# Cross attention with the sum and reciprocal of the exponentials taken two steps behind the score, and the first stage's output turned back in the banks of the query projection

## The reference, cut to what matters

```python
def _L0_xattn_ref(hidden_states_query, hidden_states_key, attention_mask, Wq, bq, Wk, bk, Wv, bv):
    q = _split_heads(hidden_states_query @ Wq.T + bq)
    k = _split_heads(hidden_states_key @ Wk.T + bk)
    v = _split_heads(hidden_states_key @ Wv.T + bv)
    scores = jnp.einsum('bhqd,bhkd->bhqk', q * scale, k)
    scores = scores + ((1.0 - attention_mask) * -10000.0)[:, None, :, :]
    probs = jax.nn.softmax(scores, axis=-1)
    ctx = jnp.einsum('bhqk,bhkd->bhqd', probs, v)
    return ctx.transpose(0, 2, 1, 3).reshape(b, lq, h * d)

def _L1_xattn_ref(query, key, value, Wq, Wk, Wv, Wo):
    # the same without biases, a causal mask over the 77 keys, and at the end
    return out @ Wo.T

x = x + _L0_xattn_ref(_layernorm(x, axis=-1), ctx_1024, mask, ...)
...
x = x + _L1_xattn_ref(_layernorm(x, axis=-1), ctx_1024, ctx_1024, ...)
```

## Time and profile before

| | |
|---|---|
| median of 3 runs | 5784.02 us (5778.58 to 5785.17) |
| the profiled execution, its own time | 5785.95 us |
| its span, first to last instruction | 5783.8 us |
| PE busy | 5318.4 us, 92% |
| DVE, ACT, POOL busy | 2616.3, 1700.1, 1270.2 us |
| `xa`, first score to last rows written | 808.6 to 1170.1 us of the span |
| `xb`, the same | 3207.1 to 3616.9 us |

### The profile page before, as it was taken

How to read it: one execution, slowest core, us unless ns; L and a number is a source line. 1 busy time by engine, 2 the same in 40 slices (tenths; PEclk the granted TensorE clock), 3 DMA queues, 4 the chain that set the end, 5 groups by cost and what they waited for, 6 DMA issues and landing times. The chain is left out here.

```text
span 5783.8 us, 76040 instructions
## 1 busy us (share of the span) xinstructions
PE 5318.4 (92%) x25936; PEld 2647.4 (46%) x25936; DVE 2616.3 (45%) x4211; ACT 1700.1 (29%) x2290; POOL 1270.2 (22%) x918
## 2 busy tenths in 40 slices
PE   8999978879999899799978899559999999999999
PEld 4444445534445444344444555424444444444444
DVE  3252336544343232254542554655555455455554
ACT  1011024412212100234321333124444444444443
POOL 1010024411112100000002121333333333333333
PEclk9999989979999899899989999579999999999999
DMA  1010021131011222598976010469598745845546
GB/s 54 8 51 0 15 73 48 40 93 43 17 29 59 93 94 87 156 210 200 218 181 220 24 45 23 151 222 341 183 327 284 243 150 157 295 152 198 180 130 236
DMA packets 437257, 770.97 MB, mean 133 GB/s; under 512 B 64386, under 2 KB 207238, under 8 KB 436564
## 3 DMA queue, kind: packets, MB, share of 16 engines
q1 hardware_dynamic: 375892, 724.24, 38.1%
q0 software_dynamic: 34304, 44.13, 3.9%
q10 hardware_dynamic: 26880, 0.19, 0.3%
HBM read 576.17 MB, written 116.79 MB: 120 GB/s over the span
## 5 line engine op out<-in xcount | busy, mean ns | idle before, releaser
L2639 PE MATMUL ex_ps<-ex_w,ex_xT 128*64 128x512 f32 x5376 | 1228.8, 599 | 18.2 <-DVE ex_w L2523 18.2
L2523 DVE COPY ex_w<-ex_shelf 128x4096 f32 x336 | 770.5, 2293 | 522.3 <-PE ex_ps L2639 370.4
L2574 ACT ACTIVATE ex_w<-ex_shelf 128x4096 f32 x168 | 607.8, 3618 | 1044.9 <-PE ex_ps L2655 1011.0
L2639 PEld LDWEIGHTS ex_ps<-ex_w,ex_xT 128*64 128x64 f32 x5376 | 373.6, 138 | 655.9 <-issue 611.6
L2655 PE MATMUL ex_ps<-ex_w,ex_hT 128*64 128x256 f32 x5376 | 610.6, 380 | 5.5 <-ACT ex_hT L2590 3.8
L2493 POOL DMA_INDIRECT out<-ex_y,ex_ix_out x168 | 287.8, 1713 | 1179.0 <-DVE ex_ix L2511 823.6
L2655 PEld LDWEIGHTS ex_ps<-ex_w,ex_hT 128*64 128x64 f32 x5376 | 389.4, 137 | 270.5 <-issue 100.2
L2476 POOL DMA_INDIRECT ex_x<-moe_xn,ex_ix x168 | 410.1, 2441 | 96.5 <-issue 51.4
L1400 PE MATMUL ff_ps<-ff_w,ff_hT 128*128 128x512 f32 x768 | 348.8, 597 | 0.8 <-DVE ff_w L1282 0.8
L1557 PE MATMUL pr_ps<-pr_w,pr_xT 128*128 128x512 f32 x768 | 337.5, 597 | 4.8 <-DMA pr_bias<-L_attn_bq 4.8
L1355 ACT ACTIVATE ff_gT<-ff_ps,ff_bet,ff_gam 128x128 f32<-128x128 f32 x384 | 144.3, 460 | 455.6 <-PE ff_ps L1408 455.6
(11 more groups left out here) (272 smaller groups left out, 7030.3 us busy)
## 6 DMA issues: line engine op xcount, KB each, us to landing
ex_shelf<-L_ffn_w SPq DMA_DIRECT2D x128, 2048.0 KB
ex_shelf<-L_ffn_wo SPq DMA_DIRECT2D x64, 2048.0 KB, 11.5
cv_gt<-cv_g SPq DMA_DIRECT2D x320, 128.0 KB, 3.3
cv_vt<-cv_v SPq DMA_DIRECT2D x256, 128.0 KB, 3.9
ff_x<-x SPq DMA_DIRECT2D x16, 1024.0 KB, 7.9
at_low<-x SPq DMA_DIRECT2D x8, 1024.0 KB, 5.7
x<-at_acc SPq DMA_DIRECT2D x8, 1024.0 KB, 4.2
xa_x<-x SPq DMA_DIRECT2D x8, 1024.0 KB, 7.7
```

Source lines behind the costliest of these rows:

```text
L2523: dve.tensor_copy(w_s[n][:, :], pick(shelf[n], buf)).then_inc(w_set[n].sem, 1)
L2574: act.activation(w_s[2][:, :], pick(shelf[2], buf), ACT.Copy).then_inc(w_set[2].sem, 1)
L2639: mm = pe.matmul(ps[q * G:(q + 1) * G, which, 0:FQ], xT[:, p % 2, k, :], wu[which][:, k, q * FQ:(q + 1) * FQ], start=k == 0, stop=k == KD - 1)
```

## The change

In both stages VectorE takes `total` of step g-2 instead of g-1 ahead of `score(g)`, and GpSimd multiplies by the reciprocal of g-2; both loops run one step longer. In `xa` alone the transposes of `put` write banks 6 and 7, in turn with `project_q`, instead of bank 5, and `add_rows` reads them there. The numbers of buffers, the instructions and their sizes are the same.

```diff
-    LT, LV, LO = 3, 4, 8
+    LS, LT, LV, LO = 2, 3, 4, 8
...
             if g >= LO and (g - LO) % 2 == 0 and (g - LO) // 2 < NT:
-                (wide if gated else side).append(("out", (g - LO) // 2))
+                wide.append(("out", (g - LO) // 2))
...
-            for g in range(G + 1):
-                if g:
-                    s3 = s_sb[:, (g - 1) % SR]
-                    pool.wait_ge(rec_done, g)
-                    pool.tensor_tensor(s3, s3, rec[:, (g - 1) % 2].unsqueeze(2).to_broadcast([P, HB, SK]), ALU.mult).then_inc(mul_done, 1)
+            for g in range(G + LS):
+                v = g - LS
+                if v >= 0:
+                    s3 = s_sb[:, v % SR]
+                    pool.wait_ge(rec_done, v + 1)
+                    pool.tensor_tensor(s3, s3, rec[:, v % 2].unsqueeze(2).to_broadcast([P, HB, SK]), ALU.mult).then_inc(mul_done, 1)
...
-                bank = 6 + wide_at["out", T] % 2 if gated else 5
+                bank = 6 + wide_at["out", T] % 2
...
-                if 1 <= g <= G:
-                    total(g - 1)
+                if LS <= g < G + LS:
+                    total(g - LS)
...
             def put(T):
                 pe.wait_ge(o_done, 2 * T + 2)
-                if gated:
-                    n = wide_at["out", T]
-                    if n >= 2:
-                        pe.wait_ge(*freed(wide, n - 2))
-                    for k in range(KD):
+                n = wide_at["out", T]
+                if n >= 2:
+                    pe.wait_ge(*freed(wide, n - 2))
+                for k in range(KD):
+                    if gated:
                         i = pe.matmul(ps[:, 6 + n % 2, :], oT[:, T % 2, k, :], wo_s[:, k, :], start=k == 0, stop=k == KD - 1)
-                else:
-                    n = side_at["out", T]
-                    pe.wait_ge(*freed(side, n - 1))
-                    for k in range(KD):
-                        i = pe.transpose(ps[:, 5, k * P:(k + 1) * P], oT[:, T % 2, k, :], ident[:, :])
+                    else:
+                        i = pe.transpose(ps[:, 6 + n % 2, k * P:(k + 1) * P], oT[:, T % 2, k, :], ident[:, :])
```

## The result

Four runs of the changed kernel gave 5697.25 to 5703.74 us, median 5702.35, against 5784.6 for the kernel before; the ratio is 0.9856, 95% interval 0.9839 to 0.9873. The profiled execution took 5697.25 us, its span is 5695.3 us.

A forecast was written before the change was run, and what follows sets the result against it. VectorE's ring was taken to bind short steps of `xa`, PE the long ones. Savings of 42.3 + 8.0 + 9.5 + 3.9 in `xa` and 6.7 in `xb`, 70.4 us, took 5784.0 to 5713.6, say 5714; range 5702 to 5742.

The forecast's parts named there:

- The ring: Short steps of `xa`: VectorE's loop through GpSimd's subtraction and the exponential makes a step 4.87 us; PE has 2.8 to 3.4.
- Put's wait: In `xa`, PE waits 11 times, 15.6 us, for the turned tile's copy ahead of put; counted inside the 46 us, not added.
- the excess: Middle chunks of `xa`: 44.55 us against the 36.9 PE needs at full clock, 7.65 us a chunk, 46 over six.
- Rival 5: A projection in `xa` would wait for rows in its bank, PE waiting at L990; given nothing of its own, no chance stated.
- The stall of 0.64 in u3: Fourth step of a middle `xa` chunk: PE stalls 0.64 us for the mask, so a chunk lasts 37.5 us.
- The deductions for a low clock: In `xa`, PE at a lowered clock takes 1.5 us off the first chunk's saving and adds 2.5 to the tail.
- The walk: The new schedule of `xa` followed step by step from PE's first score of a chunk, allowing 0.1 us for each hand-over.
- The unfavourable end: All unfavourable bounds of the stretches of `xa` and `xb` together: a gain of 33 us, time 5751.
- stalls shrink but stay: PE's 12 waits in the middle of `xb`, 14.0 us, each lose only 0.39, 4.7 in all; waits fall from 1.1 to 0.7.
- the tail loses 1.06 us: End of `xb`: rows come before the last sum, so the last step's turn_p starts later, 1.0 us lost.
- Cover of 0.24 us ahead of turn_p: Short steps of `xa`: GpSimd's product ends 0.24 us before PE reaches turn_p; cost put at nothing, bound 7 us.
- rival 4: turn_p waits for its product at L1015 in every short step of both stages: 64 us slower, 5848; chance 2%.

## Why the prediction was right and its size was not

- The ring (mask, maximum, subtraction, exponential, sum) bound the short steps of `xa`, and PE the long ones: right. With the ring open the chunk is 37.01 us, PE's own 36.9; with the sum ahead of the rows, where PE waits nowhere in these chunks, it is 36.85.
- Put's wait: right that it lies inside the excess, shown by the interaction of 18.5 us between the parts (341.4 against 413.7 - 47.2 - 6.6 = 359.9). Rival 5 (the bank move does harm) is out: once the ring is open the move brings 25 us.
- The stall of 0.64 in u3: mis-sized. It was 0.16, since I had added up VectorE's steps from durations: normalise costs 0.45 us from start to start and not 0.62, the rows 0.60 and not 0.69. A chunk became 37.01 instead of 37.5 us; 6 x 0.49 = 2.9 us, the whole miss of the middle chunks.
- The deductions for a low clock, 1.5 us in the first chunk and 2.5 in the tail: this step failed, and it is the largest of the misses. The first was carried over from the first chunk of `xb`, the second from the clock of 0.71 that the tail itself had before. Long pauses stood ahead of the slow instructions in both, in that tail one of 2.41 us and in the first chunk of `xb` these:

```profile
3210.55 0.80 PE L1006 MATMUL xb_ps<-xb_kblk,xb_qT 64*128 64x154 f32 x8 [2.66 <-DVE xb_s L856]
...
3214.69 1.40 PE L1006 MATMUL xb_ps<-xb_kblk,xb_qT 64*128 64x154 f32 x8 [2.76 <-DVE xb_s L856]
```

  In the changed kernel the pauses of the first chunk of `xa` are at most 1.0 us and those of its tail 0.6 to 0.8, and the clock is 1.00 in both stretches:

```profile
807.31 0.80 PE L1007 MATMUL xa_ps<-xa_kblk,xa_qT 64*128 64x154 f32 x8 [0.99 <-DVE xa_s L846]
...
1087.44 1.07 PE L1016 MATMUL xa_ps<-xa_ident,xa_s 128*77 128x128 f32 x8 [0.84 <-ACT xa_pT L952]
```

  The walk without the deductions (34.4 and 14.3) meets the measured 33.95 and 14.06. These 4 us and the 2.9 are 6.9 of the 8.9 by which the terms fell short; the rest is the last chunk (0.7), the walk of the first (0.4) and of the tail (0.2) and `xb` (0.7).
- Not all of the distance is the forecast's. With the 8.9 us put right it would say 5704.7, inside the range; the measured 5700.7 is 4 us lower still, and nothing in the traces ties these 4 us to the change. The interval of the ratio is 10 us to either side.
- The range was built on bounds of both signs, but its lower end allowed only 12 us, and the errors did not cancel: each of the five stretches gained more than was forecast. The unfavourable end was also added up wrongly. The bounds given are 35.3, 4, 6 and 0 in `xa` and -1.0 in `xb`, which make a gain of 44 us (5740), not 33 (5751).
- `xb`: stalls shrink but stay (7.8 us, 12 times), the tail loses 1.06 us against 1.0: right. The sum of 7.4 against 6.7 hides two misses: the middle gained 6.2 instead of 4.7, the first chunk 0.85 instead of 1.8, at a clock that is 0.83 there, lower than before (0.87).
- Cover of 0.24 us ahead of turn_p: it held in the middle chunks. In the last chunk of `xa`, where the steps are shortest, GpSimd's product starts 0.40 us after the mask instead of 0.16, since the subtraction ahead of it ends only then, and in three steps turn_p follows its score by 0.86 us instead of 0.73: rival 4's mechanism at a price of 0.13 us each. One more step of lag costs about 225 us against the changed kernel.

## What to carry to other kernels

When an in-order engine sits in a ring with others, take what nobody waits for out of the ring by lagging it one more step, and walk the new schedule by start-to-start distances, not durations. Look for the waits that the ring was hiding: the bank move was worth 6.6 us alone and 25 beside the other part, a third of the gain. Ask of a low clock where it falls: in a step that waits for another engine it cost nothing. Lag as little as possible: one step too many made a ring of its own, slower than the one removed.

## What was not expected of the hardware

The clock of a stage that no edit touches differs between kernels. The 32 gate products at the start of the routing stage took 7.09 us in the profile before and 3.79 in the one after, though both follow 28 us of idling and the same transposes. From the first transpose to the end of the products the granted clock is 0.50 before and 0.81 after:

```profile
3648.91 7.09 PE L2356 MATMUL ro_ps<-ro_gate,ro_xT 128*128 128x64 f32 x32 [0.69 <-ACT ro_xT L219]
```

```profile
3563.50 3.79 PE L2354 MATMUL ro_ps<-ro_gate,ro_xT 128*128 128x64 f32 x32 [0.69 <-ACT ro_xT L219]
```

That stage took 186.6 to 197.6 us over all executions. These products explain little of it: in the two executions of the sum ahead of the rows they took 3.79 us both times, and the stage 191.6 and 196.5. What sets it stays open; it is why small differences were read from the stages here and not from the program's time.
